# Paged attention loop: mask product over 128 rows with zero-padded token matrices, newest keys' masked values made by ScalarE instead of GpSimd

## What is computed

```
q, k, v = x @ Wq, x @ Wk, x @ Wv          # 8 query heads, 4 key groups, 32 features each
q, k = rope(rms(q), pos), rope(rms(k), pos)   # pos = kv_lens + token
cache[block_tables, pos] = k, v           # the 32 newest keys and values of each sequence
scores = q @ k_all * 256 ** -0.5
allowed = (kpos <= pos) & (kpos > pos - 128)
p = softmax(where(allowed, scores, -inf))
out = (p @ v_all) @ Wo
```

## Time and profile before

| | |
|---|---|
| median of 3 runs | 561.83 us (560.03 to 563.0) |
| the profiled execution, first to last instruction (span) | 556.4 us |
| around the span, by the median | 5.4 us |
| TensorE matmul busy | 482.5 us, 87% |
| TensorE weight loads busy | 362.9 us, 65% |
| VectorE busy | 368.8 us, 66% |
| ScalarE busy | 252.8 us, 45% |
| GpSimd busy | 261.7 us, 47% |
| mean granted TensorE clock | 0.951 |

### The profile page before, as it was taken

One profiled execution on the slowest core, in us unless ns is written; L12 is line 12 of the kernel. 1 busy time (PEld: TensorE's weight loads), 2 busy tenths in 40 slices (PEclk: granted clock), 3 DMA queues, 4 the chain that ended last, 5 costly groups with the idle time before them and its releaser, 6 DMA issues. The chain is left out here.

```text
span 556.4 us, 10841 instructions
## 1 busy us (share of the span) xinstructions
PE 482.5 (87%) x4169; PEld 362.9 (65%) x4169; DVE 368.8 (66%) x808; ACT 252.8 (45%) x551; POOL 261.7 (47%) x240
## 2 busy tenths in 40 slices
PE   2897799999899899999887989966999979699963
PEld 0576448888688688877665444754777756489952
DVE  2666667888488687874567664495778976744423
ACT  7267755344243333434277343336565544234430
POOL 5045534565253377868465000047886117336650
PEclk9999999999999999999899998975899999989985
DMA  5463845000000012213000000087100002598217
GB/s 175 181 247 126 356 147 151 1 0 2 0 1 0 1 58 70 63 57 115 2 2 3 1 1 1 16 300 292 27 27 19 3 3 99 179 319 270 102 60 226
DMA packets 24723, 51.53 MB, mean 93 GB/s; under 512 B 4264, under 2 KB 16705, under 8 KB 23520
## 3 DMA queue, kind: packets, MB, share of 16 engines
q1 hardware_dynamic: 18704, 40.62, 21.2%
q0 software_dynamic: 5968, 10.22, 5.9%
HBM read 43.99 MB, written 12.37 MB: 101 GB/s over the span
## 5 line engine op out<-in xcount | busy, mean ns | idle before, releaser
L755 PE MATMUL ps<-x_split,gate_up_split 128*128 128x512 f32 x384 | 96.4, 393 | 0.1
L755 PEld LDWEIGHTS ps<-x_split,gate_up_split 128*128 128x128 f32 x384 | 72.1, 188 | 17.2 <-issue 1.5
L2194 POOL DMA_INDIRECT wbig<-new_kv,prepi x40 | 43.2, 1081 | 75.0 <-DMA new_kv<-work 63.8
L946 POOL TENSOR_TENSOR gate_up_split<-wbig,gate_up_split 128x768 fp32r<-128x768 f32 (+1 forms) x24 | 41.5, 1730 | 52.4 <-ACT gate_up_split L884 52.3
L866 DVE TENSOR_TENSOR hidden_split<-work,hidden_split 128x512 fp32r<-128x512 f32 x34 | 37.6, 1107 | 23.1 <-ACT hidden_split L935 23.1
L2126 POOL DMA_INDIRECT chosen<-work,wbig x31 | 30.5, 984 | 31.3 <-ACT work L2105 16.3
L777 PE MATMUL ps<-hidden_split,down_split 128*128 128x512 f32 x160 | 42.5, 395 | 2.6 <-issue 1.4
L935 ACT ACTIVATE hidden_split<-work 128x512 fp32r<-128x512 f32 x34 | 21.4, 629 | 49.7 <-DVE work L861 49.7
L952 POOL TENSOR_TENSOR down_split<-wbig,down_split 128x384 fp32r<-128x384 f32 (+1 forms) x24 | 29.1, 1213 | 25.9 <-ACT down_split L891 25.8
L2194 POOL DMA_INDIRECT wbig<-in_cache_dram,prepi x32 | 33.5, 1047 | 7.6 <-issue 7.2
L777 PEld LDWEIGHTS ps<-hidden_split,down_split 128*128 128x128 f32 x160 | 29.8, 188 | 10.6 <-issue 4.2
(11 more groups left out here) (353 smaller groups left out, 1164.8 us busy)
## 6 DMA issues: line engine op xcount, KB each, us to landing
work<-in_wE_dram SPq DMA_DIRECT2D x1, 5376.0 KB, 19.7
wbig<-in_wF_dram SPq DMA_DIRECT2D x3, 1664.0 KB, 6.8
sorted<-wmid SPq DMA_DIRECT2D x1, 3999.0 KB, 16.1
wbig<-in_wG_dram SPq DMA_DIRECT2D x1, 3072.0 KB, 10.5
wbig<-in_wE_dram SPq DMA_DIRECT2D x6, 384.0 KB, 3.8
wbig<-chosen SPq DMA_DIRECT2D x8, 256.0 KB, 5.0
wbig<-sorted SPq DMA_DIRECT2D x1, 1935.0 KB, 13.0
wmid<-in_wE_dram SPq DMA_DIRECT2D x5, 384.0 KB, 7.3
```

The source lines that it names most:

```text
L755: mm = nc.tensor.matmul(o, self.gus[:, w % 2, a, 2 * m + k, :], self.xs[:, b, k, n * HALF:(n + 1) * HALF], start=(k == 0 and a == b), stop ...
L946: nc.gpsimd.tensor_tensor(self.gus[:, k % 2, 1, 0:self.gu_chunks], self.gate_up[:, :, j * P:(j + 1) * P], self.gus[:, k % 2, 0, 0:self.gu_ ...
L2194: return nc.gpsimd.indirect_dma_start(dst, None, table, bass.IndirectOffsetOnAxis(ap=rows.bitcast(U32), axis=0), **({} if bound is None el ...
```

## The change

The token matrix for the mask product is no longer one matrix of which 32 rows are used; there are four, one for each sequence of a group, with all rows but the sequence's 32 set to zero, and the product runs over all 128 rows of them and of the masks. Three of these matrices lie in a part of the work buffer that becomes free after the attention of the first two layers, so GpSimd makes them there, in two products, after a wait for that attention, instead of the one copy. The masked values of the newest keys are made by ScalarE, four activations per group (copy with a column of "quad" as scale), in its order behind the exponentials of the group's last sequence; GpSimd's queue loses last_values and its waits. The semaphores count accordingly (page_token 2, page_vlast four per group).

```diff
--- before.py
+++ after.py
@@ -1381,7 +1381,9 @@
 
         page_free = MOE_COLS + wP_d.shape[1]
         masks = split_buf("masks", wbig_at, page_free, B // 4 * NKEY).rearrange("p (q j) -> p q j", q=B // 4)
-        token_r = split_buf("token_rows", wbig_at, page_free + B // 4 * NKEY, P)
+        token_low = split_buf("token_rows", work_at, 10880, 3 * P).rearrange("p (j q) -> p j q", j=3)
+        token_high = split_buf("token_rows_last", wbig_at, page_free + B // 4 * NKEY, P)
+        token_r = [token_low[:, 0], token_low[:, 1], token_low[:, 2], token_high]
         assert page_free + B // 4 * NKEY + P <= wbig.shape[1]
         pst = small_buf(B * 6).rearrange("p (b x) -> p b x", b=B)
         oT = cut(wmid, 3072, 2048).rearrange("p (h t) -> p h t", h=2)
@@ -1480,7 +1482,7 @@
                     tr.then_inc(sem("page_qt"), 1)
             pe.wait_ge(sem("page_qm"), 16)
             pe.wait_ge(sem("page_table"), 10 + B // 4)
-            pe.wait_ge(sem("page_token"), 1)
+            pe.wait_ge(sem("page_token"), 2)
 
             def keys(q4):
                 pe.wait_ge(sem(f"overlay{q4 % 4}"), 16 * 5 * (q4 // 4 + 1))
@@ -1494,9 +1496,8 @@
                 pe.wait_ge(sem("page_kT"), 2 * (b // 4) + 2)
                 if b >= 2:
                     pe.wait_ge(sem("page_exp"), 2 * b - 2)
-                j = slice(32 * (b % 4), 32 * (b % 4) + 32)
-                nc.tensor.matmul(ps[:, 2 + b % 2, 0:2 * NKEY].rearrange("p (a j) -> p a j", a=2), token_r[j, :],
-                                 masks[j, b // 4, :].unsqueeze(1).to_broadcast([32, 2, NKEY]), start=True, stop=False)
+                nc.tensor.matmul(ps[:, 2 + b % 2, 0:2 * NKEY].rearrange("p (a j) -> p a j", a=2), token_r[b % 4],
+                                 masks[:, b // 4, :].unsqueeze(1).to_broadcast([P, 2, NKEY]), start=True, stop=False)
                 for a in range(2):
                     mm = nc.tensor.matmul(ps[:, 2 + b % 2, a * NKEY:(a + 1) * NKEY],
                                           qmask[:, b, 2 * a:2 * a + 2, :, :].rearrange("p g h t -> p (g h t)"),
@@ -1522,7 +1523,7 @@
             def values(q4):
                 pe.wait_ge(sem("page_lT"), q4 + 1)
                 pe.wait_ge(sem("page_pT"), 4 * q4 + 4)
-                pe.wait_ge(sem("page_vlast"), q4 + 1)
+                pe.wait_ge(sem("page_vlast"), 4 * q4 + 4)
                 if q4:
                     pe.wait_ge(sem("page_o"), q4)
 
@@ -1685,6 +1686,14 @@
                 nc.scalar.activation(kT[:, :, P:NKEY], ps[:, 1, 0:P].rearrange("p (b j) -> p b j", b=4), ACT.Copy)\
                     .then_inc(sem("page_kT"), 1)
 
+            def last_values(q4):
+                act.wait_ge(sem(f"overlay{q4 % 4}"), 16 * 5 * (q4 // 4 + 1))
+                if q4 >= 2:
+                    act.wait_ge(sem("page_pv"), q4 - 1)
+                for j in range(4):
+                    nc.scalar.activation(vlast[:, q4 % 2, j], kv[:, B + q4, P:2 * P], ACT.Copy, scale=const("quad")[:, j:j + 1])\
+                        .then_inc(sem("page_vlast"), 1)
+
             keep_keys(0)
             for b in range(B):
                 act.wait_ge(sem("page_max"), b + 1)
@@ -1705,6 +1714,8 @@
                     keep_keys(b // 4 + 1)
                 if b % 4 == 2 and b > 2:
                     keep_output(b // 4 - 1)
+                if b % 4 == 3:
+                    last_values(b // 4)
                 if b == 25:
                     route_exponents(act, 0)
             moe.first_weights(act)
@@ -2285,23 +2296,18 @@
             pool.wait_ge(sem("ffn_down_done"), ffn_b.count("down_done", 16))
             nc.gpsimd.memset(vpar.rearrange("p g a h d -> p (g a h d)"), 0.0).then_inc(sem("zeroed"), 1)
             nc.gpsimd.memset(pdiag.rearrange("p r h q -> p (r h q)"), 0.0).then_inc(sem("zeroed"), 1)
-            nc.gpsimd.tensor_copy(token_r, const("token")).then_inc(sem("page_token"), 1)
             pool.wait_ge(sem("cached"), 16 * B)
             att_b.gpsimd(pool)
+            pool.wait_ge(sem("att_pv_done"), 2 * NT)
+            nc.gpsimd.tensor_tensor(token_low, const("token").unsqueeze(1).to_broadcast([P, 3, P]),
+                                    const("quad")[:, 0:3].unsqueeze(2).to_broadcast([P, 3, P]), ALU.mult)\
+                .then_inc(sem("page_token"), 1)
+            nc.gpsimd.tensor_tensor(token_high, const("token"), const("quad")[:, 3:4].to_broadcast([P, P]), ALU.mult)\
+                .then_inc(sem("page_token"), 1)
 
             pool.wait_ge(sem("prep_step"), N_PREP)
             order = [t for q4 in range(B // 4) for t in [B + q4] + list(range(4 * q4, 4 * q4 + 4))]
             pool.wait_ge(sem("page_new"), 32)
-
-            def last_values(q4):
-                pool.wait_ge(sem(f"overlay{q4 % 4}"), 16 * 5 * (q4 // 4 + 1))
-                if q4 == 0:
-                    pool.wait_ge(sem("fold_done"), 1)
-                if q4 >= 2:
-                    pool.wait_ge(sem("page_pv"), q4 - 1)
-                nc.gpsimd.tensor_tensor(vlast[:, q4 % 2], kv[:, B + q4, P:2 * P].unsqueeze(1).to_broadcast([P, 4, P]),
-                                        const("quad").unsqueeze(2).to_broadcast([P, 4, P]), ALU.mult)\
-                    .then_inc(sem("page_vlast"), 1)
 
             pool.wait_ge(sem("page_rot"), 2)
             for n, t in enumerate(order):
@@ -2309,10 +2315,6 @@
                 if q4 >= 4 and n % 5 == 0:
                     pool.wait_ge(sem(f"overlay{q4 % 4}"), 16 * 5)
                 gather(kv[:, t, :], new_kv, new_rowi[:, t:t + 1], T - 1).then_inc(sem(f"overlay{q4 % 4}"), 16)
-                if n % 5 == 4 and n >= 10:
-                    last_values(n // 5 - 2)
-            last_values(B // 4 - 2)
-            last_values(B // 4 - 1)
             moe.gpsimd(pool)
             send_half(pool, 0)
             send_half(pool, 1)
```

## The result

The changed kernel takes 552.5 us, the median of its runs (550.97 to 552.94); the kernel before takes 562.3 us beside it (560.03 to 563.0). The ratio of the times is 0.984, with a 95% interval of 0.981 to 0.988; the medians over all runs stand 9.8 us apart. In a second series the same kernel came to 0.983 (0.979 to 0.988). By the ratio it is faster by 8.9 us on the 561.8 us that the forecast started from; 7.9 were forecast. The profiled execution's span is 549.0 us; 548.5 was forecast.

The account below looks back on a forecast made before the run. In the page loop TensorE was busy but waiting around the mask product, and VectorE, held by GpSimd, decided the rest. Gains of 2.5 + 4.0 + 1.4 = 7.9 us gave 553.9 us from 561.8, range 551.2 to 559.0.

Parts of the forecast that it names:

- Scores: TensorE in the page loop: with 128 rows a sequence's scores cost 0.40 us less, 0.20 in one of four sequences.
- scores of 0.68 us in the chain: Sign to look for in the page loop: a sequence's mask product and four passes take 0.68 us instead of 1.08.
- Rival (a): Page loop: the number type change, not the rows, makes the idle times; gain 5.4 us, 556.4 us; chance 0.12.
- The beginning: First four sequences of the page loop, at TensorE's half clock: shorter scores gain 1.1 us, bounds 0 and 2.3.
- GpSimd's holds: Page loop: without GpSimd's eight masked-value products, VectorE's products are no longer held; 4.0 us gained.
- part 1: Mask product over 128 rows in the page loop: 1.1 + 1.2 + 0.2 = 2.5 us gained.
- Rival (d): Page loop: VectorE's long instructions are not GpSimd's doing; only the 128 rows gain, 559.3 us; chance 0.05.
- ScalarE's copies: Page loop: four copies per group at 0.26 us each, 1.05 us, hidden within up to 1.1 us; cost 0.
- Rival (b): Page loop: ScalarE's copies cost their upper bound, 2.9 us in seven groups; gain 5.0, 556.8 us; chance 0.08.
- Rival (e): Page loop: ScalarE becomes the bound, price per instruction, four copies 2.8 us; 4.0 us slower, 565.8 us; chance 0.05.
- The last group: End of the page loop: L946 starts 1.05 us later and no longer holds VectorE's last normalisation; 1.4 us gained.
- Rival (c): Behind the loop: gain lost to a transfer or longer low TensorE clock; 2 us or less left, about 560; chance 0.10.

Follow-up runs that it names:

- e3: The changed kernel with the mask product over 64 rows instead of 128; ratio 0.991 to the kernel before.
- e2: ScalarE's copies as in the changed kernel, but the mask product back on 32 rows; ratio 0.992 to the kernel before.
- e7: The changed kernel plus eight spare GpSimd products at the removed ones' places, writing where nobody reads; ratio 0.992 to the kernel before.
- e8: The changed kernel with ScalarE's four copies split, two at a group's second sequence and two at its fourth; ratio 0.983 to the kernel before.
- e6: The changed kernel with the last group's copies moved behind the split of the shared expert's weights; ratio 0.986 to the kernel before.
- e1: The changed kernel with the masked values given back to GpSimd, the mask product still over 128 rows; ratio 0.997 to the kernel before.
- e10: The changed kernel with 128 rows in the mask product for sequences 0 to 3 only, 32 from then on; ratio 0.989 to the kernel before.

## Why the prediction was right, and where it was off

The number and its sign came out, and most terms did; two were off in size, and their errors are of opposite signs.

**Scores.** Right in the sum. None of the idle time that came with 32 rows is left around L1499. From the start of one mask product to the start of what follows the scores, and from the pair of turned blocks ahead to the product, TensorE's timelines show, before:

```profile
409.03 0.38 PE L1511 MATMUL ps<-small,wmid 128*128 128x128 f32 x2
409.34 0.41 PE L1498 MATMUL ps<-masks,token_rows 32*128 32x320 f32 x1
...
411.17 0.41 PE L1498 MATMUL ps<-masks,token_rows 32*128 32x320 f32 x1
...
412.16 0.38 PE L1511 MATMUL ps<-small,wmid 128*128 128x128 f32 x2
```

and after:

```profile
407.76 0.39 PE L1499 MATMUL ps<-masks,token_rows 128*128 128x320 f32 x1
407.99 0.70 PE L1502 MATMUL ps<-work 128*128 128x160 f32 x4
408.53 0.42 PE L1512 MATMUL ps<-small,wmid 128*128 128x128 f32 x2
...
412.79 0.38 PE L1512 MATMUL ps<-small,wmid 128*128 128x128 f32 x2
412.93 0.39 PE L1499 MATMUL ps<-masks,token_rows 128*128 128x320 f32 x1
```

Ahead of it 0.31 us became 0.14, and from it to the block behind the scores 0.99 became 0.77: 0.39 us less per sequence, where 0.40 was forecast. The product's own part is 0.23 us and not 0.14, but the gap ahead of it is shorter by as much. So the sign "scores of 0.68 us in the chain" did not come: the chain has 0.39 + 0.54 = 0.93 us for them, where it had 1.08, and the rest of the 0.39 us lies in the gap ahead. Rival (a), the number type, fell with e3 and with these rows.

The Trainium skill, "TensorEngine Tiling (Array Packing)", Key Properties, has the rule by which TensorE drains when the tiling mode changes. The rows agree, for 64 rows as for 32, and here the idle time is 0.16 us behind the product at every sequence and 0.17 us ahead of it at 18 of 32. The prediction had it on both sides at every such switch. So TensorE's part of a group shrinks by less than the prediction's 1.4 us; the sum does not change by that, for it let only 0.40 us count.

**The beginning.** Wrong in size: the term was 1.1 us and 2.86 came. The step that failed is "Four sequences run at that clock". It took the lower level, 1.2 GHz, as given for the first four sequences, with a shorter product in it. But the clock rose 5.7 us behind the first key transpose and not 10.4; the 1.8 us that the term lacks I put down to that. The mask product of the third sequence, the last that the changed kernel begins at the low clock, bears this out (timelines of the matmuls, before and after):

```profile
388.12 0.63 PE L1498 MATMUL ps<-masks,token_rows 32*128 32x320 f32 x1
```

```profile
388.86 0.51 PE L1499 MATMUL ps<-masks,token_rows 128*128 128x320 f32 x1 [0.24 <-ACT wmid L1704]
```

Behind the first key transpose that is 6.04 and 5.45 us, only 0.59 gained; the other 2.27 come between there and the maximum of sequence 3, 5.01 us before and 2.74 after. (With 64 rows, where no idle time went and the clock rose 1.1 us sooner, the stretch up to that maximum gained 0.46 us.) The windows, before and then after:

```profile
387.00:390.00 3.00, 3.00 (x10) 2.36 (x11) 1.13 (x4) 1.54 (x8) 2.58 (x3) 0.50 0.09 25
390.00:393.00 3.00, 3.00 (x14) 2.39 (x13) 1.46 (x5) 1.63 (x6) 2.48 (x3) 0.58 0.19 52
```

```profile
387.00:390.00 3.00, 2.76 (x13) 2.19 (x12) 1.67 (x6) 1.67 (x8) 2.32 (x3) 0.65 0.28 80
390.00:393.00 3.00, 2.73 (x21) 2.44 (x21) 2.78 (x10) 2.44 (x12) 2.39 (x3) 1.00 0.18 40
```

That 128 rows bring an early rise is shown: all eleven profiles with 128 rows in the first four mask products have it at 5.6 to 6.9 us, e3 with 64 at 9.3, e2 and the kernel before at 10.4. Where the low clock begins differs too: 13.5 us ahead of the first key transpose in the kernel before, e2 and e7, and 11.2 to 11.4 in e3 and the changed kernel. Like with like, 128 rows move the rise by 3.5 us (e7's 6.9 against e2's 10.4) or 3.6 (the changed kernel's 5.7 against e3's 9.3), and the 1.1 us between 64 and 32 rows can be that beginning alone. Why the rows matter is open. In the 5.7 us behind the first key transpose TensorE's matmuls were busy for 4.84 us before and 4.61 after, its weight loads for 3.56 and 3.84.

**GpSimd's holds.** Right with part 1 in place. The four long instructions and those of the middle groups were to give 4.0 us. By stretches, with part 1's share in them: maximum 3 to 6, 1.26 forecast and 1.08 measured; the three middle groups 1.86 and 1.69; from the maximum of 19 to that of 31, where VectorE is the bound, 2.24 (three of the long ones and 0.2 of part 1) and 2.22. Outside the terms 0.24 came at sequence 7. Rival (d) fell with e7. What the prediction did not see is how far the two parts lean on each other: it had 2.5 us for part 1 and 5.4 for the rest, and alone they are worth 3.5 and 4.2 us in the loop, with 1.8 us more for both at once. That the whole comes out near the sum is in part luck.

**ScalarE's copies.** A little too cheap. The timeline of ScalarE:

```profile
407.18 1.27 ACT L1694 ACTIVATE wmid<-wbig,small 128x128 f32<-128x128 f32 x4
408.35 0.38 ACT L1704 ACTIVATE wmid<-ps,prep 128x160 f32<-128x160 f32 x1
```

Four copies take 408.35 - 407.18 = 1.17 us, 0.29 each, against 0.26 and 1.05 forecast and 1.1 hidden. It is just over the edge, as VectorE's timeline above has it: the reciprocal at 409.23 stands 0.50 us behind its maximum of 408.73, where 0.41 is the usual distance. The scores at 409.34 wait for the exponentials behind the copies as well, and the chain that ended last goes that way:

```profile
408.45 0.75 ACT wmid L1704 x4
409.20 0.14 issue
409.34 0.39 PE ps L1499
```

So one of the signs by which the prediction was to be wrong, "if VectorE begins to wait for ScalarE in the loop", did come, in small: e8, which splits the copies, gets 0.11 us of a middle group back, which would be under 1 us in all. The column as scale was priced from an exponential "less 0.03 for 32 fewer columns"; it costs the exponential's full distance. Rival (b) had the mechanism and three times the price. Rival (e) fell: a copy of 128 columns takes 0.39 us, not the 0.68 to 0.73 of 512 columns.

The Trainium skill, "ScalarE: Activation LUTs", What ACT_TABLE_LOAD costs, adds about 93 ns for a column operand, from which the prediction had an estimate of 0.29 us per copy and 1.17 per group. The trace has just these two numbers.

**The last group.** Right: 1.4 forecast, 1.41 measured, and shown by e6. The 0.2 us by which it was to fit were 0.3: the normalisation, begun at 446.63, is through at 447.20, and L946 starts at 447.53.

**The padded matrices.** Right at 0. GpSimd's two products are in the linear attention stage. This is the first; the second begins at 312.54 us and takes 0.40 us:

```profile
311.76 0.83 POOL L2302 TENSOR_TENSOR token_rows<-small 128x384 fp32r<-128x384 f32 x1 [6.68 <-PE ps L414]
```

and VectorE's instruction beside the second, which reads PSUM, took 0.69 us, as it does in the kernel before.

**The sum.** The loop gained 9.5 us and not 7.9: 1.8 too little at the beginning, 0.2 unforeseen at sequence 7, 0.2 too much at sequences 3 to 6, 0.2 too much in the middle. Of the 9.5, 8.9 show in the times. The span of one execution shows 7.4, for the stages ahead of the loop differ by a microsecond or two from execution to execution; that the forecast span of 548.5 us was met to 0.5 us is in part luck. Rival (c) is there in small: 0.8 us is lost behind the loop, and I put it down to the lower clock, whose stretch caught 1.4 us more of the experts' matmuls.

## What to carry to other kernels

Read GpSimd's rows beside VectorE's: a long VectorE instruction that ends just behind a GpSimd one was held by it, and a faster kernel can meet it elsewhere, as e1 did, so the GpSimd work has to go as well. A lone matmul of few rows between full ones is worth padding with zeros, for the idle time beside it goes; here that is 2.5 us in the loop even behind its beginning (e10's 66.26 against 63.79), and more with the earlier clock. Work moved to another engine has the room between two answers that this engine owes, here 1.1 us per group, whatever its busy share; 1.17 us was just too much, and a second 1.17 was lost in full in the middle stretch, but not where VectorE was the bound.

## What the runs showed of the hardware that I had not expected

- At the start of the page loop the granted clock rises to 2.4 GHz at 5.6 to 6.9 us behind the first key transpose with mask products of 128 rows, at 9.3 us with 64 and at 10.4 us with 32, for the same columns, and TensorE's matmuls were not busier before the early rise (4.61 of 5.7 us, against 4.84). That 64 rows differ from 32 is not shown. Four products of 128 rows, one per sequence, are enough (e10).
- A hold lasts as long as GpSimd's instruction, or as several of them that stand back to back: 1.35 us beside one product, 2.45 us beside two, 0.66 us beside a copy of 0.62 us, for VectorE products of 64 columns that take 0.23 to 0.28 us alone. VectorE's instruction is held even where it begins 0.2 to 0.3 us ahead of GpSimd's (e7, e1), and its reads of PSUM are not held (0.42 us beside a product as alone).
- One idle time of 2.86 us on TensorE, made by such a hold, was followed by the lower clock (0.62 as the mean of the next 3 us, e1).
